# Two-layer cross-attention and mixture-of-experts kernel: the score maxima are filled bank pair by bank pair, with matmuls of the two row groups in turn

## The reference

```python
x = x + _L0_xattn_ref(_layernorm(x), ctx, ctx, ...)   # 16 windows of 128 queries, 16 heads of 16, keys of the same window
x = x + _L0_ffn_ref(_layernorm(x), ...)               # 16 experts, top 2, and a shared gated layer of 512
x = x + _L1_xattn_ref(_layernorm(x), ctx, ...)        # 8 batches, 256 queries against 256 keys, 16 heads of 16
x = x + _L1_ffn_ref(_layernorm(x), ...)               # 8 experts of 1024, top 2
```

## Time and profile before

| | us |
|---|---|
| three executions | 1073.47, 1074.34, 1064.76 |
| their median | 1073.47 |
| the profiled execution, its own time | 1076.29 |
| its span in the trace | 1074.6 |
| TensorE matmuls busy | 794.8 |
| VectorE busy | 595.4 |
| ScalarE busy | 372.2 |
| mean granted clock of TensorE | 0.853 of full speed |

### The profile page before, as it was taken

One profiled execution on the slowest core, in us unless ns is written; L12 is line 12 of the kernel. 1 busy time (PEld: TensorE's weight loads), 2 busy tenths in 40 slices (PEclk: granted clock), 3 DMA queues, 4 the chain that ended last, 5 costly groups with the idle time before them and its releaser, 6 DMA issues.

```text
span 1074.6 us, 23613 instructions
## 1 busy us (share of the span) xinstructions
PE 794.8 (74%) x8366; PEld 599.1 (56%) x8367; DVE 595.4 (55%) x1396; ACT 372.2 (35%) x735; POOL 232.2 (22%) x248
## 2 busy tenths in 40 slices
PE   3968996587968999827969999650029999999900
PEld 1535653543637888714526666450029999899800
DVE  1546775347434777637666887469325445545513
ACT  2214554132222332311225666434224444444400
POOL 2100111003841222176100000004731101100065
PEclk9986998588989999969957999755559999999965
DMA  5992222372742333249950000446722233223234
GB/s 178 124 135 41 74 71 93 129 254 93 241 155 69 104 103 106 88 125 165 123 61 2 3 2 3 163 159 225 271 76 66 67 69 74 68 65 75 61 108 132
DMA packets 83804, 113.40 MB, mean 106 GB/s; under 512 B 16512, under 2 KB 64512, under 8 KB 83744
## 3 DMA queue, kind: packets, MB, share of 16 engines
q1 hardware_dynamic: 69712, 76.72, 28.3%
q0 software_dynamic: 12112, 34.49, 10.8%
q10 hardware_dynamic: 1920, 1.34, 0.4%
HBM read 65.19 MB, written 28.18 MB: 87 GB/s over the span
## 4 chain that ended last, share of the span: by engine, by line
PE 57%; DVE 15%; POOL 11%; issue 7%; DMA 5%; ACT 2%; SPq 1%; ACTq 0%; DVEq 0%; POOLq 0%
PE bank L725 16%; PE bank L738 12%; POOL slot_in L1361 7%; PE bank L533 5%; PE bank L554 3%; POOL arena L1382 3%; PE bank L502 3%; PE bank L710 2%; DVE neg_max L1067 2%; PE bank L463 2%; PE bank L474 2%; PE bank L520 2%; DMA arena<-in_ctxT 2%; DVE stats L1004 2%; DVE xn_buf L1014 2%
## 5 line engine op out<-in xcount | busy, mean ns | idle before, releaser
L725 PE MATMUL bank<-arena 128*128 128x128 f16 x3024 | 302.6, 220 | 3.4 <-DVE arena L1240 3.4
L738 PE MATMUL bank<-arena 128*128 x1224 | 281.1, 273 | 3.7 <-DVE arena L1248 2.0
L725 PEld LDWEIGHTS bank<-arena 128*128 x3024 | 264.5, 98 | 19.7 <-issue 4.1
L1361 POOL DMA_INDIRECT slot_in<-arena,slot x64 | 81.8, 1278 | 303.3 <-DVE slot L1208 284.3
L1067 DVE TENSOR_REDUCE neg_max<-bank 128x2 f32<-128x512 f32 (+1 forms) x192 | 125.0, 685 | 29.4 <-PE bank L502 28.1
L972 ACT ACTIVATE arena<-bank,arena 128x128 f32<-128x128 f32 x312 | 85.4, 381 | 123.9 <-DMA arena<-in_exp_b 107.9
L738 PEld LDWEIGHTS bank<-arena 128*128 128x128 f16 x1224 | 119.4, 98 | 12.1 <-issue 11.3
L1369 POOL DMA_DIRECT2D arena<-slot_in x87 | 47.9, 551 | 291.7 <-PE bank L710 273.7
L855 ACT ACTIVATE arena<-bank 128x1024 f32<-128x1024 f32 x96 | 96.5, 1026 | 11.2 <-PE bank L520 10.8
L710 PE MATMUL bank<-consts,arena 128*128 128x128 f32 x174 | 35.1, 286 | 74.9 <-DVE arena L1235 68.7
L502 PE MATMUL bank<-arena 48*128 48x128 f16 (+1 forms) x512 | 69.7, 271 | 11.8 <-DVE bank L1105 7.6
(11 more groups left out here) (126 smaller groups left out, 1089.9 us busy)
## 6 DMA issues: line engine op xcount, KB each, us to landing
arena<-arena SPq DMA_DIRECT2D x96, 128.0 KB, 6.7
arena<-slot_in POOLq DMA_DIRECT2D x87, 128.0 KB, 2.4
slot_out<-arena SPq DMA_DIRECT2D x87, 128.0 KB, 1.7
arena<-in_exp_up SPq DMA_DIRECT2D x16, 512.0 KB, 4.1
slot_in<-arena POOLq DMA_DIRECT2D x16, 384.0 KB, 2.9
arena<-in_exp_up SPq DMA_DIRECT2D x5, 1024.0 KB, 7.8
arena<-in_exp_dn SPq DMA_DIRECT2D x5, 1024.0 KB, 8.3
arena<-in_exp_b SPq DMA_DIRECT2D x39, 128.0 KB, 3.4
```

The source lines that it names most:

```text
L725: last = mm(upP[u][:, m // (UB // 2), m % (UB // 2) * P:(m % (UB // 2) + 1) * P], weights(e, 0, w, k * UPW[l] + m * P, P), rowsT[u][x][:, ...
L738: last = mm(yP[u], hidT[u][x][:, k], weights(e, 1, w, k * D, D), start=n == 0, stop=n == n_second - 1)
L1361: pool.indirect_dma_start(slot_in, bass.IndirectOffsetOnAxis(ap=slot[:, i, t:t + 1], axis=0), xn_all[l][:, t], None).then_inc(s["scattered ...
```

## The change

Pairs of banks are filled together. `first_head(l, m)` gives the first head of bank `m`: banks 2j and 2j + 1 now hold heads of group 0 and group 1 in both layers. In layer 0 the assignment of heads to banks stays (0 to 3, 4 to 7, 8 to 11, 12 to 15); in layer 1 it becomes 0 1, 4 5, 2 3, 6 7, 8 9, 12 13, 10 11, 14 15. The matmuls of a pair are issued in turn, one of each group, and before the pair TensorE waits until both banks of the pair before are read. `SPREAD` has only even entries now.

```diff
-    SPREAD = [[0, 1, 3, 4, 4], [0, 2, 3, 4, 5, 7, 8]]
+    SPREAD = [[0, 2, 2, 4, 4], [0, 2, 2, 4, 4, 6, 8]]
...
+        def first_head(l, m):
+
+            n = H // (4 * KV[l])
+            return m // 2 // (4 // n) * 8 + m // 2 % (4 // n) * n + m % 2 * 4
+
...
-                    for m in range(lo, hi):
-                        after(pe, s["max_read"], i * NM + m - 1)
+                    for m in range(lo, hi, 2):
+                        after(pe, s["max_read"], i * NM + m)
                         for hh in range(HM):
-                            h = m * HM + hh
-                            last = mm(mx[m % 2][:, hh * KW * P:(hh + 1) * KW * P], q_stack[group_rows(h, KR), at(h), ds(i * P, P)],
-                                      k_stack[group_rows(h, KR), at(h), ds(keys(i), KW * P)], start=True, stop=True)
-                        last.then_inc(s["max_mm"], 1)
+                            for g in range(2):
+                                h = first_head(l, m + g) + hh
+                                last = mm(mx[g][:, hh * KW * P:(hh + 1) * KW * P], q_stack[group_rows(h, KR), at(h), ds(i * P, P)],
+                                          k_stack[group_rows(h, KR), at(h), ds(keys(i), KW * P)], start=True, stop=True)
+                                if hh == HM - 1:
+                                    last.then_inc(s["max_mm"], 1)
...
-                        v.tensor_reduce(neg_max[u][:, column(m * HM):column(m * HM) + 2 * HM - 1:2], mx[m % 2].rearrange("p (h k) -> p h k", h=HM),
+                        v.tensor_reduce(neg_max[u][:, column(first_head(l, m)):column(first_head(l, m)) + 2 * HM - 1:2], mx[m % 2].rearrange("p (h k) -> p h k", h=HM),
```

## The result

| | before | after |
|---|---|---|
| median of four executions, us | 1071.99 | 1093.86 |
| lowest and highest | 1064.76, 1074.34 | 1089.75, 1096.44 |
| span of the profiled execution | 1074.6 | 1092.9 |
| ratio after to before, 95% interval | | 1.0212 (1.0152 to 1.0272) |

The account below looks back on a forecast made before the run. The prediction took VectorE's reads on the path to set layer 0's pace, with TensorE and VectorE level in layer 1. Terms 0.6 + 0.1 + 7.6 + 3.5 - 1.3 + 7.3 = 17.8 us on the 1073.47 median gave 1091.3, range 1079 to 1101.

Parts of the forecast that it names:

- Alternation: Maxima matmuls of L502: eight alternating between row groups take the 0.39 us that four in one group took.
- Layer 0, steady: Layer 0's steady step: second reduce before the divide and 0.03 us at the add, +0.63 us, 6.06 instead of 5.43.
- Against the latter: Argument against a clock staying low through both attention stages (62 us, 1154 us in total, chance 0.02).
- L548's idle for `att` grows from 0.24 to about 0.9 us: Expected sign in layer 0's steady step: TensorE's transposes wait longer for the divide's result, 0.9 us instead of 0.24.
- Layer 1, steady: Layer 1's steady step: last pair waits for both reads, L509 starts later, +0.61 us per step, 12 steps +7.3 us.
- Cold steps: Layer 1's steps at 1.2 GHz: TensorE is the bound and paired fills save 1.3 us in step 1, nothing in step 0.
- Rival C: Attention stages: clock rises later; one step more in each gives 1096.5 us, all steps 1154; chance 0.10 and 0.02.
- Filling up: Maxima blocks before step 0: refilling waits for both reads of a pair, +3.5 us in layer 1, +0.6 in layer 0.
- A: Both attention stages: TensorE is the bound, so paired fills save 15.9 us, giving 1057.6 us; chance 0.04.
- B: Steady steps of both layers: moved reads mostly hidden, a third of the delay shows, +7.6 us, 1081 us; chance 0.12.
- a clock that differs through a stage: Sign of being wrong, in any stage: the granted clock differs through it; no size given.
- The 1073.5 us: Whole kernel by the packing rule alone: emptying banks is the bound, faster fills bring and cost nothing, median stays 1073.5 us.

## Why the prediction was right, and where not

The forecast, 1091.3 us within 1079 to 1101, holds the measured 1093.86; slower by over 1% had the chance 0.84. The sum of the terms was 17.8 us; the profiles show 18.3. The mechanism of the steady steps was right, but the closeness of the two sums is luck, because errors of several us met: 6.0 us of falls that had no term, 2.6 us by which the cold step of layer 1 came out better than its term, and 2.8 us by which the rest of the program, which the change does not touch, was shorter in the second profile. The two attention stages alone grew by 21.1 us.

*Alternation.* "Eight then need what four needed, 0.39 us" held (0.39). The step that failed is the reading of it as an effect of the alternation: the run with the pairs in sequence takes 0.41. The eight matmuls of L502 before L548, four of one group and then four of the other, lasted 0.40 us before the change already. That row of the timeline of the kernel before:

```profile
128.69 0.40 PE L502 MATMUL bank<-arena 48*128 48x128 f16 x8
```

I had judged the overlap from L520, which alternates, and did not ask what this row says of two blocks in a row.

*Layer 0, steady.* Forecast +0.63 us by the second reduce before the divide and 0.03 at the add; measured 6.00 instead of 5.43, +0.57. Undone alone on VectorE, it is 5.45. The term was right. What it lacked is the clock: I had written "Against the latter: the long projection, values and scores are unchanged" of a clock that stays low, and had considered only a late rise, not a fall at full pace. Four falls are 6.0 us, more than any error in my arithmetic. My own line "L548's idle for `att` grows from 0.24 to about 0.9 us" named the stop behind which it happens; it measured 1.11.

*Layer 1, steady.* Forecast +0.61, measured 8.13 against 7.53, +0.60, by the named waits: 0.32 us before the last fill (forecast about 0.15) and 0.35 at L516. I counted the wait for both banks as the cause. The run without pairs shows 8.08, so the place of two reads behind the add is enough for it. That the pair's wait costs there what slower fills would cost otherwise is argued from the rows of the two runs; no run has fast fills in these places without the wait.

*Cold steps.* The term -1.3 us for layer 1's second step was mis-sized; it measured -3.9, and for another reason. I had put it down to paired fills, but without pairs and with the new places the step took 8.60 and 8.59 us. What shortens it is the clock, which reached 2.4 GHz about 1.4 us into the step (the stretch 579 to 580 us above) instead of 0.8 us before its end. Rival C expected the opposite sign. Why the clock rises earlier with these places stays open. Pairs save something in the step before, at 1.2 GHz: 11.10 us against 11.46 without them.

*Filling up.* Forecast +3.5 and +0.6 us. Measured 1.8 + 1.8 in layer 1; in layer 0 0.6 for tile 0, and 0.2 and 0.4 in the two differences after it. The 0.2 is no more than chance: the unchanged layer 0 took 4.83 us from tile 0 to 1 in the run with layer 1 alone, against 4.07.

*Rivals.* A falls: TensorE had less to do (17.65 of 20 us busy instead of 19.50) and the kernel was slower, with its waits for VectorE longer. B falls by the step times. C came in another form: the clock rose no later, but it fell at full pace, and over the steps from tile 4 on its mean in layer 0 was 0.91 instead of 1.00. The prediction had named a clock that differs through a stage as a sign of being wrong.

The Trainium skill's rule (TensorEngine Tiling (Array Packing), "PSUM Bottleneck") goes with the steady steps: fills of 0.39 us instead of 0.61 in layer 1, together with the pair's wait, left them no shorter (8.13 and 8.08 us). The 1073.5 us that it would give alone did not come, since it leaves out where the reads stand.

## What to carry to other kernels

Where two engines meet several times in a step, ask of every moved instruction which wait it stands in front of: here one reduce of 0.69 us on the wrong side of a divide cost nearly half of the loss (9.9 of 21.9 us at the medians, the falls of the clock included), while the feature that the change was built around, alternating row groups, did nothing. Wherever a change makes TensorE wait longer in a pattern that repeats, read the granted clock of each step after it, since idle time can cost twice, as the four steps of about 7.5 us did here. And a saving on an engine that is 97% busy by its records is none until a row shows that nothing waits for another engine in that place.

## What the runs showed of the hardware

- With an idle stretch of 1.0 to 1.1 us in each step, TensorE's granted clock fell to 1.2 GHz in four of eleven steps of layer 0, which took 1.5 us longer. It did so in the same four steps in the profiles of three kernels with pairs, and in one step in that of the kernel without pairs. With useless matmuls in the stretch (16 records, about 0.6 us) it stayed up.
- The rise of the clock came a step earlier or later by small changes in order: layer 1's second step (tile 2 to 3) took 12.65, 8.77, 8.71 or 8.59 us, the same step of layer 0 8.07, 7.86, 7.49 or 6.55.
- Matmuls of 48 rows in two row groups overlapped even when four of one group were issued before four of the other: 0.41 us for eight, against 0.39 in turn, where four of one group alone took 0.39. Of 256 columns, four in two groups took 0.39 us and four in one group 0.61.
